# A routed feed-forward, attention, feed-forward block: sorting the tokens in two parts

## The reference

```python
x = L0_attn_x                                     # (16, 512, 128) float32: 8192 tokens of 128
x = x + 0.5 * ffn(layernorm(x))
x = x + attn(layernorm(x))
x = x + 0.5 * ffn(layernorm(x))

def ffn(x):                                       # 8 experts, 128 -> 512 -> 128
    h   = mod(int32(x_flat[:, 0] + x_flat[:, 1]), 8)
    sel = [h, (h + 1) % 8]                        # two experts per token, each with weight 1/2
    out = sum over e of 0.5 * (e in sel) * (relu(x_flat @ W1[e] + b1[e]) @ W2[e] + b2[e])

def attn(x):                                      # projections, a linear recurrence over 512 steps
    t   = (x @ W_U * W_V).sum(-1) + x @ W_toP
    lam = sigmoid(sigmoid(x @ W_F) @ W_lam);  u = t @ B_mat
    s_t = lam_t * s_(t-1) + u_t
    return (t + s @ C_mat) @ W_fromP
```

## Time and profile before

| | |
|---|---|
| median of 3 runs | 600.19 us (599.95 to 601.44) |
| profiled execution, first to last instruction (span) | 598.6 us |
| PE busy | 514.1 us (86%) |
| DVE busy | 432.9 us (72%) |
| ACT, POOL busy | 296.2, 321.1 us |
| first feed-forward, first matmul of tile 0 | at 63.03 us |
| second feed-forward, first matmul of tile 0 | at 386.82 us |

### The profile page before, as it was taken

How to read it: one execution, slowest core, us unless ns; L and a number is a source line. 1 busy time by engine, 2 the same in 40 slices (tenths; PEclk the granted TensorE clock), 3 DMA queues, 4 the chain that set the end, 5 groups by cost and what they waited for, 6 DMA issues and landing times.

```text
span 598.6 us, 15962 instructions
## 1 busy us (share of the span) xinstructions
PE 514.1 (86%) x5269; PEld 437.2 (73%) x5269; DVE 432.9 (72%) x1026; ACT 296.2 (49%) x494; POOL 321.1 (54%) x410
## 2 busy tenths in 40 slices
PE   0278899999999999956799836999999999999990
PEld 0136599999999999942466614689999999999980
DVE  6899677777777777746876779677777777777760
ACT  2384655555555556412988400155555655555540
POOL 3014847777777767350016610447777677777543
PEclk9996999999999999997999967699999999999996
DMA  9980111112111112109003380111121111112100
GB/s 244 328 340 11 41 34 50 47 47 50 48 51 43 51 41 53 31 30 266 16 1 72 72 142 1 28 38 46 51 50 48 44 46 47 48 51 51 36 24 18
DMA packets 37850, 40.96 MB, mean 68 GB/s; under 512 B 5813, under 2 KB 30731, under 8 KB 37266
## 3 DMA queue, kind: packets, MB, share of 16 engines
q1 hardware_dynamic: 27698, 21.65, 13.5%
q0 software_dynamic: 9088, 17.87, 11.5%
q10 hardware_dynamic: 992, 0.44, 0.3%
HBM read 23.00 MB, written 17.83 MB: 68 GB/s over the span
## 4 chain that ended last, share of the span: by engine, by line
PE 69%; DVE 14%; issue 5%; DMA 3%; ACT 3%; POOL 3%; SPq 2%; POOLq 0%; DVEq 0%
PE ps L774 19%; PE ps L756 10%; PE ps L758 10%; PE ps L757 10%; PE ps L776 10%; PE ps L792 2%; SPq L366 2%; PE ps L680 2%; PE ps L728 2%; DMA X<-in_L_attn_x 1%; DVE X L1122 1%; DVE bn L1101 1%; POOL G L478 1%; DVE onehot_b L987 1%; PE ps L836 1%
## 5 line engine op out<-in xcount | busy, mean ns | idle before, releaser
L1047 DVE SCALAR_TENSOR_TENSOR hlo<-ps,hhi 128x1024 f16<-128x1024 f32 x144 | 174.1, 1209 | 103.0 <-ACT hhi L586 103.0
L586 ACT ACTIVATE hhi<-ps 128x1024 f16<-128x1024 f32 x144 | 145.7, 1012 | 170.1 <-PE ps L758 170.1
L774 PE MATMUL ps<-w2s,hhi 128*128 x1136 | 202.3, 273 | 0.0
L776 PE MATMUL ps<-w2s,hlo 128*128 x1136 | 194.9, 219 | 0.0
L478 POOL DMA_INDIRECT G<-rows,places x142 | 141.9, 1000 | 88.2 <-issue 40.2
L756 PE MATMUL ps<-xhi,w1s 128*128 128x256 f16 (+1 forms) x736 | 168.0, 248 | 3.9 <-DVE xlo L1041 2.1
L758 PE MATMUL ps<-xhi,w1s 128*128 128x256 f16 (+1 forms) x736 | 168.0, 248 | 0.0
L757 PE MATMUL ps<-xlo,w1s 128*128 128x256 f16 (+1 forms) x736 | 167.9, 248 | 0.0
L774 PEld LDWEIGHTS ps<-w2s,hhi 128*128 128x128 f16 x1136 | 111.1, 98 | 12.1
L776 PEld LDWEIGHTS ps<-w2s,hlo 128*128 128x128 f16 x1136 | 111.1, 98 | 1.3
L486 POOL DMA_INDIRECT x1d<-O,places x71 | 71.3, 1004 | 41.6 <-issue 29.1
(11 more groups left out here) (240 smaller groups left out, 509.5 us busy)
## 6 DMA issues: line engine op xcount, KB each, us to landing
rows<-X SPq DMA_DIRECT2D x2, 2080.0 KB, 12.0
rows<-X SPq DMA_DIRECT2D x4, 1040.0 KB, 7.6
X<-in_L_attn_x SPq DMA_DIRECT2D x8, 512.0 KB, 8.0
X<-x1d SPq DMA_DIRECT2D x8, 512.0 KB, 7.4
G<-rows,places POOLq DMA_INDIRECT x142, 2.6
w1r<-in_L_ffn_W SPq DMA_DIRECT2D x1, 2048.0 KB, 11.3
x1d<-O,places POOLq DMA_INDIRECT x71, 2.3
out<-O,places POOLq DMA_INDIRECT x71, 2.3
```

What stands on the lines that cost most here:

```text
L586: nc.scalar.activation(hhi[tile.k][e][:, :, 0:tile.cols], H[e][:, :, 0:tile.cols], ACT.Relu).then_inc(hi_done[e], 1)
L774: nc.tensor.matmul(Y[tile.k][:, s, :], hhi[tile.k][e][:, c, tok], w, start=first, stop=False, skip_group_check=True)
L776: ins = nc.tensor.matmul(Y[tile.k][:, s, 0:P], hlo[tile.k][e][:, c, tok], wh, start=False, stop=(e == 1 and c == CH - 1), skip_group_check ...
L1047: v.scalar_tensor_tensor(out=hlo[tile.k][e][:, :, c], in0=H[e][:, :, c], scalar=0.0, in1=hhi[tile.k][e][:, :, c], op0=ALU.max, op1=ALU.sub ...
```

## The change

The sort is made in two parts. The first 48 of the 64 token columns are sorted alone; they give 17 tiles of one class, which can run when only they are known (15 of them stand at the front of the new order of tiles, the other two among the rest). The other columns, and what the first part left over, are sorted while those tiles run. The helpers on DVE are now generators, and `between` puts up to six of their steps after `low(j, 0)` and up to six at the end of each tile, all that are left where a stage ends. Stages, by tile: classes of the rest 0 to 2, ranks and places 4 and 5, one-hots 6 to 9, lists and tables 11 and 12. PE counts after step 3 and multiplies after steps 7 to 10, 16 matmuls each (64 again, since leftovers are in all columns, now 37 blocks wide). Positions come by a code per class that is looked up, no longer by shifts over 8 x 64 arrays. In the middle, DVE does the third group's classes and those of 48 columns after add_out(5), and PE's count for them stands between out_s(5) and the projections of q = 7. POOL does two groups, and its scatters at the end no longer wait for `h_ready[1]`. The sum for W2 still stands ahead of the last 16 columns of the first part, and b2's sum comes earlier on POOL (after the count).

```diff
+    FIRST = (48, 48)
+    PURE1 = [FIRST[r] * P // FT - (E - 1) for r in range(2)]
+    LEAD = PURE - (MIXED - 1)
+    REST_AT = [min(p, LEAD) for p in PURE1]
...
         def layout(j):
-            m = max(0, j - (NJ - 3 * MIXED) + 1) // 3
-            is_pure = j < NJ - 3 * MIXED or (j - (NJ - 3 * MIXED)) % 3 < 2
-            return (j - m, True) if is_pure else (PURE + m - 1, False)
+            i = j - LEAD
+            if i < 0 or i % 2:
+                return (j if i < 0 else LEAD + i // 2), True
+            return PURE + i // 2, False
...
+        STEPS = 6
+        COUNT_AT = (3, 3)
+        SELECT_AT = ((6, 7, 8, 9), (6, 7, 8, 9))
...
+            for c in range(FIRST[0] // XC):
+                load_x(c)
+            sp.wait_ge(x_in[FIRST[0] // XC - 3], 16)
             sp.dma_start(w1r[:], W1.rearrange("e d f -> d e f")).then_inc(w_in[0], 16)
...
+            sp.wait_ge(stats_ready, 1)
+            sp.dma_start(*rows_of(0, FIRST[0])).then_inc(rows_first[0], 16)
+            for c in range(FIRST[0] // XC, NX):
+                load_x(c)
...
-            pool.wait_ge(sel_b, len(PIECES))
+            pool.wait_ge(rank_ready, 1)
             g.tensor_tensor(b2t[:, 0:E - 1, :], b2r[:, 0:E - 1, :], b2r[:, 1:E, :], ALU.add)
...
+                def put(j):
+                    first_scatter(j)
+                    pool.wait_ge(o_ready, Tile(r, j).done())
+                    scatter(Tile(r, j))
+
+                for j in range(NJ):
+                    tile = Tile(r, j)
+                    if j + AHEAD < NJ:
...
+                        gather(tile + AHEAD)
+                        if j >= BEHIND:
+                            pool.wait_ge(h_ready[1], tile.done())
+                            put(j - BEHIND)
+                for j in range(NJ - AHEAD - BEHIND, NJ):
+                    put(j)
...
+            def count(k, c0, c1):
+                before, in_all = rank_banks(c1 - c0)
+                pe.wait_ge(oh_ready, k)
+                nc.tensor.matmul(before, after16[:], oh[:, :, c0:c1], start=True, stop=True)
+                nc.tensor.matmul(in_all, ones16[:], oh[:, :, c0:c1], start=True, stop=True).then_inc(rank_ready, 1)
...
                 for j in range(-1, NJ + 1):
+                    if j == REST_AT[r]:
+                        pe.wait_ge(table_ready, 2 + 2 * r)
                     if 0 <= j < NJ:
                         held[j] = load(Tile(r, j).at)
                     step(Tile(r, j))
                     held.pop(j - 1, None)
+                    if j == COUNT_AT[r]:
+                        count(2 + 2 * r, FIRST[r], NT)
+                    for g in range(NT // GRP):
+                        if j == SELECT_AT[r][g] + 1:
+                            select(2 * r + 1, g)
...
+                if q == NPAIR - 2:
+                    count(3, 0, FIRST[1])
             out_x(NPAIR - 1)
             out_s(NPAIR - 1)
-            sort(1)
-            warm(20, 4)
+            warm(24, 4)
+            for g in range(FIRST[1] // GRP):
+                select(2, g)
+            warm(24, 4)
...
+                stages = [(0, COUNT_AT[r] - 1, rest_classes(r)), (COUNT_AT[r] + 1, min(SELECT_AT[r]) - 1, rest_ranks(r))]
+                stages += [(SELECT_AT[r][g], SELECT_AT[r][g], one_hots(2 * r + 1, g)) for g in range(NT // GRP)]
+                stages += [(max(SELECT_AT[r]) + 2, max(SELECT_AT[r]) + 3, rest_routes(r))]
+
+                def between(j, n, all_of_it):
+                    for start, end, steps in stages:
+                        if start <= j <= end:
+                            for k, _ in enumerate(steps):
+                                if k + 1 >= n and not (all_of_it and j == end):
+                                    break
...
                     low(tile, 0)
+                    between(j, STEPS, False)
...
                     if j >= 1:
                         collect(tile + -1)
+                    between(j, STEPS, True)
...
+                if q == NPAIR - 2:
+                    for g in range(2):
+                        dve.wait_ge(ln3_ready[g], 1)
+                    for g in range(2, FIRST[1] // (2 * XC)):
+                        run(own_classes(g))
+                    run(classify(0, FIRST[1]))
+            run(ranks(3, 0, FIRST[1]))
+            run(assign_first(1))
+            for g in range(FIRST[1] // GRP):
+                run(one_hots(2, g))
             add_out(NPAIR - 1)
-            sort(1)
+            run(route(2))
+            run(tables(2))
             ffn(1)
```

More of the change, by code:

```diff
@@ L349, in chain @@
[L349 to L360, removed]
+            ch.mark(v.tensor_tensor(l_a[:, s], X[:, s, 0], X[:, s, 1], ALU.add))
+            yield
+            ch.wait()
+            ch.mark(v.tensor_tensor(l_b[:, s], l_a[:, s], l_m[:, s], ALU.subtract))
@@ new lines, in class_sum, with run, rank_banks @@
+            yield
+            ch.wait()
+            ins = v.tensor_tensor(cls_s[:, s], l_b[:, s], l_y[:, s], ALU.mult)
+            if done is not None:
+                ins.then_inc(done, 1)
+            else:
+                ch.mark(ins)
+                yield
+                ch.wait()
+        def run(steps):
+            for _ in steps:
+                pass
+        def rank_banks(w):
+            if 2 * E * w <= 512:
+                return ps[:, 7, 0:E * w], ps[:, 7, E * w:2 * E * w]
+            return ps[:, 1, 0:E * w], ps[:, 7, 0:E * w]
@@ new lines, in first_sort @@
+            def first_sort():
+                count(1, 0, FIRST[0])
+                pe.wait_ge(sq_done, 1)
+                nc.tensor.matmul(ps[:, 6, 0:2], ones[:], sq[:, 0:2], start=True, stop=True).then_inc(sum_pe, 1)
+                warm(8, 0)
+                w_times(0)
+                w_times(1)
+                for e in range(2, EARLY):
+                    w_times(e)
+                    w_less(e - 2)
+                w_less(EARLY - 2)
+                w_less(EARLY - 1)
+                for g in range(FIRST[0] // GRP):
+                    if g == FIRST[0] // GRP - 1:
@@ new lines, in summed, with look_up @@
+            def summed(z, w):
+                ch.mark(v.tensor_tensor_scan(z[:, 1:E + 1], ones_row[:, 0:E], w, 0.0, ALU.mult, ALU.add))
+            def look_up(w):
+                ch.mark(v.tensor_tensor(wide(posv, w), oh[:, :, 0:w], each(code8[:], w), ALU.mult))
+                yield
+                ch.wait()
+                with nc.allow_low_precision(reason="one code of eight is not zero"):
+                    ch.mark(v.tensor_reduce(code_i[:, 0:w], wide(posv, w).rearrange("p e t -> p t e"), AX.X, ALU.add))
+                yield
+                ch.wait()
@@ new lines, in rest_ranks, with rest_routes @@
+            def rest_ranks(r):
+                yield from ranks(2 + 2 * r, FIRST[r], NT)
+                yield from assign_rest(r)
+            def rest_routes(r):
+                yield from route(2 * r + 1)
+                yield from tables(2 * r + 1)
+            run(classify(0, FIRST[0]))
+            run(ranks(1, 0, FIRST[0]))
+            run(assign_first(0))
+            dve.wait_ge(iota_ready, 1)
+            for g in range(FIRST[0] // GRP):
+                run(one_hots(0, g))
+            run(route(0))
@@ L1031, in _ @@
+            run(tables(0))
             w2_low(0)
```

675 lines of the change are left out of this document (460 added, 215 removed).

## The result

The change makes the kernel slower: **619.94 us** (median of 4 runs, 618.32 to 620.71) against 600.17 in the runs beside it; ratio 1.0324, 95% interval 1.0306 to 1.0342. The forecast was 612 with a range of 600 to 621; the result lies beyond the 605 to 619 that the forecast itself had in that range, and inside the 617 to 623 of its rival B. The profiled execution spans 616.5 us against 598.6, 17.9 more; it is the fastest of the four, 1.6 us under their median.

The account below looks back on a forecast made before the run. PE bounds both feed-forwards, DVE's sort chain the stretches without tiles. Against 598.6 us: -9.9 - 4.2 - 4.4 + 9.6 + 10.3 + 9.0 + 2 = +12.4, 611.0; with 1.6 for the median, 612 (range 600 to 621).

Parts of the forecast that it names:

- rival B: Clock halves in PE's stall before tile 7: 2.7 to 5.5 us per feed-forward, 617 to 623 in all; chance 0.2.
- Start, -9.9: Before tile 0: fewer X chunks and a shorter DVE sort bring layer1 to 53.1, a gain of 9.9 us.
- Ends, -4.2: Ends of both feed-forwards: last scatters stop waiting on later tiles, gaining 2.1 us each.
- Middle, -4.4: Between the feed-forwards: scan of q = 7 comes 13.1 us later, but less sorting follows; first gather 4.4 us earlier.
- Tiles, PE, 4.8 each: PE's gapless queue in the tiles: 64 sorting matmuls and two counts add 4.8 us per feed-forward.
- Tiles, DVE, 10.3 and 9.0: DVE's bursts of steps delay x_low, so PE waits 10.3 us in the first feed-forward, 9.0 in the second.
- Rival A: DVE's steps between tiles disappear in its idle time; 591 us as a median, faster; chance 0.14.
- the forecast's 27.8 us: Total of DVE's sorting steps put between the tiles of the first feed-forward, against 1.43 us spare per tile.
- What was to be seen: Profile signs: layer1 near 53, periods 7 and more at sorting matmuls, 9.6 before tile 7, PE idle 334 to 344.
- worst stall: Steps flushed at the end of tile 5 make PE stand still for 4.1 us before tile 7.
- The 2 for small steps beside POOL: Allowance of 2 us in the tiles for DVE's small steps taking longer beside POOL's gathers.

Follow-up runs that it names:

- tail_alone: The kernel before, with only the end scatters' waits on the hidden layer of later tiles removed; 597.72 us.
- count_late: The changed kernel with PE's count for the second sort moved from behind out_s(5) to behind out_s(6); 611.11 us.
- select_twice: The changed kernel with every sorting matmul in the tiles issued twice, the second into an unread part of the bank; 629.10 us.
- steps_in_one: The kernel before plus 23 chained scratch steps on DVE behind one tile's collect in each feed-forward; 610.72 us.
- steps_in_five: The kernel before plus 23 chained scratch steps on DVE, spread over five tiles of each feed-forward; 600.88 us.
- spread: The changed kernel with the one-hots in tiles 7 to 10 instead of 6 to 9; 611.21 us.
- all_three: The changed kernel with PE's count moved behind out_s(6), one-hots in tiles 7 to 10, and the first slot of steps behind x_low and residual; 596.63 us.
- load_first: The changed kernel with count behind out_s(6), one-hots in tiles 7 to 10, first slot behind x_low, residual's address loaded before the slot, residual after; 596.03 us.
- spread_slot: The changed kernel with one-hots in tiles 7 to 10 and the first slot of steps behind x_low(j+1), ahead of residual; 611.07 us.
- b2_later: Like all_three, with POOL's sum of b2 moved behind the two gathers of tile 0; 598.38 us.

## Why the prediction was right in direction and too low

The traces hold 5.5 us more than the forecast (17.9 against 12.4), the median 1.6 more since the profiled execution was the fastest.

- **Start, -9.9: mis-sized.** The chain by ACT to the sum of W2 was right to 0.2 us. "From there ... everything follows as before" failed: the twelve warm-up matmuls took 4.45 at the lower clock, not 2.76 as in the kernel before. Short by 1.6.
- **Ends, -4.2: mis-sized.** tail_alone gives 2.6 by itself; the last scatters did not start right behind collect.
- **Middle, -4.4 with the first end's -2.1: -7.6 measured.** From T35 to the scan of q = 7 it took 10.5 longer (360.35 less 262.28 against 339.65 less 252.06; forecast 13.1 less 2.1), from there to T0 18.1 less (forecast 17.6). count_late confirms that PE's blocked queue held the scan; without it the gain is 8 more.
- **Tiles, PE, 4.8 each: right in size, by luck in its reason.** The four tiles with 16 sorting matmuls took 5.1 and 5.2 more; select_twice pays for as many again. The price of one had been halved on account of the clock, and it was the narrower matmul that halved it (last section).
- **Tiles, DVE, 10.3 and 9.0: right in mechanism, 1.3 too high in the first and right in the second.** PE waited 11.6 and 10.3 for x_low, of which 2.6 and 1.3 stand in for waits that the kernel before has: 9.0 is added in each. That small steps fit or do not fit tile by tile was the reason, and steps_in_one against steps_in_five shows it by itself. Rival A (they vanish in idle time) falls with this: the idle sum was never what counted. (The steps of the forecast's 27.8 us add up to 28.1; nothing rests on the difference.)
- **What was to be seen** came, nearly: layer1 of tile 0 at 54.69 where 53.1 was forecast, ACT's sum as the releaser, periods of 6.7 to 7.1 where sorting matmuls stand, PE idle in the middle (342.7 to 352.9), and one long period, 11.17 where 9.6 was forecast.
- **The clock: the step that failed.** The sum had it at nothing and left it to rival B, with a chance of 0.2. It costs 1.4 behind the worst stall in each feed-forward. In the first it was also at 0.50 behind the wait of 3.57 before tile 1: from T1 to T3, waits taken off, the changed kernel took 11.14 and the kernel before, at a clock of 1.00, 8.94, so 2.2 more. As terms of T0 to T15: waits -1.3 and 0, clock +3.6 and +1.4, sorting matmuls +0.3 and +0.4, a rest that I cannot assign +0.6 and +1.0, together 6.0, less the 2 that were added for DVE beside POOL: 4.0. With 1.6 of the start, 0.8 of the second end, -1.1 of the middle and 0.2 of the later tiles this is the 5.5. The worst stall itself was right (4.31 for 4.1).
- **The 2 for small steps beside POOL: luck.** It would have to show in PE's waits, and these came out 1.3 below the forecast without it. It made up for a part of what the clock cost. (residual's waits without a releaser, 1.3 and 0.9 in the two stretches of the changed kernel, are a delay on DVE that the forecast did not have; as far as they reach PE, they are inside its waits.) The range held because its upper part had been given to rival B.

What remains open: the 1.1 us in the middle of steps_in_one and steps_in_five, how much of the 8.7 of spread is variation from run to run, and why the clock fell behind one wait of 2.30 and not behind the other.

Against tail_alone (597.72), which contains none of the sorting in two parts, all_three and load_first win 1.1 and 1.7 us: about that is what the sort in two parts is worth once its count, its bursts and residual's load are in better places. (The intervals of all_three and tail_alone overlap; those of load_first and tail_alone do not.) By the stretches of all_three, it does not pay in the first feed-forward (T0 8.1 earlier, but T0 to T15 9.3 and T15 to T35 1.4 longer), and it does in the second (T35 to T0 is 118.1 instead of 133.4, T0 to T15 9.9 longer).

## What to carry to other kernels

Work that is put between the tiles of a loop must be counted tile by tile, ahead of the instruction that the bounding engine waits for; the spare time of all tiles together says nothing, since 4.8 us of steps cost 4.4 to 5.2 in one tile and 0.3 over five. In an in-order queue, look at what stands behind each new wait (two matmuls cost 8 us) and at register loads: residual's cost nothing ahead of a chain of short steps and about 4 us of waits per feed-forward behind such chains. An edit without effect may be two effects that cancel; look at the waits before dropping it.

## What the runs showed of the hardware

- Sorting matmuls hardly depend on the clock. In the changed kernel sixteen of 34 columns took 1.28 from 41.68 (granted clock 0.50 from 41 to 43) and 1.27 from 374.38 (clock 1.00 from 374 to 376). The forecast had halved 0.142, which was for 71 columns at 0.50, on account of the clock, and so met the 0.075 of 37 columns in the tiles; by these rows the narrower matmul is what made it cheaper, not the clock.
- Behind waits of 2.85 (steps_in_one) and 4.31 (the changed kernel) in the midst of dense tiles the granted clock was 0.50 to 0.58. Behind a wait of 2.30 it was 0.52 in the first feed-forward of spread and 1.00 in the second; behind 1.77 in spread_slot it stayed at 1.00. One fall cost 1.4 to 1.65 in such tiles.
- DVE and POOL hold each other up: a cast of 128x68 took 2.79 beside POOL's sum of b2 in b2_later, and 0.20 in all_three. The Trainium skill ("SBUF — State Buffer", section "Who interferes with whom") says that the two share a pair of ports and that one can block the other for a whole instruction; the 2.79 agrees in its end, since the cast was done at 50.10 and the longer instruction of POOL's sum ran from 47.95 to 50.04; the cast had begun at 47.31, ahead of it, and this part is not explained. In all_three a step of 8 columns on DVE took 1.61 beside the same sum, and both ended within 0.02 us (45.89 and 45.87).
